# Selective scan of a two-layer adaLN block: TensorE turns the next state's increments ahead of the step's sum

## The reference, cut to what matters

```python
def _selective_scan(u, dt, A, Bm, Cm, Dvec):
    dA = jnp.exp(dt[..., None] * A)
    dBu = dt[..., None] * Bm[:, :, None, :] * u[..., None]
    def step(h, xs):
        dA_t, dBu_t, C_t = xs
        h = dA_t * h + dBu_t
        y = jnp.einsum('bdn,bn->bd', h, C_t)
        return (h, y)
    ...
    return jnp.swapaxes(ys, 0, 1) + u * Dvec
# per layer, after the scan:
    y = y * _silu(z)
    return jnp.einsum('bld,od->blo', y, W_out)
```

## Time and profile before

| what | value |
|---|---|
| median of 3 runs | 775.03 us (768.9 to 779.73) |
| the profiled execution | 776.74 us, span 774.8 us |
| busy over the span | TensorE 83%, VectorE 76%, ScalarE 64%, GpSimd 59% |
| scans, line 1644 | 128, 289.6 us in two groups |
| sums, line 1130 | 512 matmuls, 239.1 us |
| increments, line 1150 | 688 transposes, 91.8 us in two groups |
| C multiplication, line 468 | 128, 301.9 us in two groups |

### The profile page before, as it was taken

The page is one execution under the profiler, slowest core; times in us unless marked ns, Lnnn a source line. Parts: engine busy times, 40 slices in busy tenths (PEclk is TensorE's granted clock), DMA queues, the critical chain, the costliest instruction groups (busy, mean ns, idle before and its releaser), DMA issues. The chain is left out here.

```text
span 774.8 us, 8846 instructions
## 1 busy us (share of the span) xinstructions
PE 642.5 (83%) x2913; PEld 394.4 (51%) x2913; DVE 589.9 (76%) x799; ACT 496.1 (64%) x931; POOL 456.3 (59%) x260
## 2 busy tenths in 40 slices
PE   4946677796699999999986699999999962399993
PEld 2344456432445565555532445565555551389992
DVE  6794986554799999999765799999999858844521
ACT  3553334468799988889668799988989543033321
POOL 1236653100388989879700398989879715058866
PEclk9885877679699999999999699999999965599998
DMA  5000000000223222323100223223322181013333
GB/s 194 0 3 1 0 1 0 1 2 7 80 81 104 89 95 85 106 91 93 48 3 9 78 84 102 88 98 85 104 93 93 46 300 54 1 22 42 39 32 27
DMA packets 30780, 48.05 MB, mean 62 GB/s; under 512 B 3736, under 2 KB 12328, under 8 KB 30224
## 3 DMA queue, kind: packets, MB, share of 16 engines
q1 hardware_dynamic: 25600, 44.45, 18.0%
q0 software_dynamic: 5136, 3.05, 3.6%
HBM read 42.98 MB, written 4.49 MB: 61 GB/s over the span
## 5 line engine op out<-in xcount | busy, mean ns | idle before, releaser
L468 POOL TENSOR_TENSOR hc_all<-hs_all,c_row 128x1024 f32<-128x1024 f32 x88 | 207.3, 2368 | 133.2 <-DVE hs_all L1644 129.9
L1130 PE MATMUL ps<-hc_all,ident 128*128 128x512 f32 x512 | 239.1, 598 | 3.8 <-POOL hc_all L468 2.7
L1644 DVE TENSOR_TENSOR_SCAN hs_all<-da,ps 128x1024 f32<-128x1024 f32 x88 | 198.2, 2271 | 17.1 <-ACT da L794 9.6
L794 ACT ACTIVATE da<-big,a_neg 128x511 f32<-128x511 f32 x256 | 169.2, 709 | 30.5 <-DVE w_ffn L1644 27.6
L1130 PEld LDWEIGHTS ps<-hc_all,ident 128*128 128x128 f32 x512 | 90.2, 192 | 87.5 <-issue 74.2
L468 POOL TENSOR_TENSOR hc_all<-w_ffn,c_row 128x1024 f32<-128x1024 f32 x40 | 94.6, 2365 | 31.7 <-DVE w_ffn L1644 31.7
L1644 DVE TENSOR_TENSOR_SCAN w_ffn<-da,ps 128x1024 f32<-128x1024 f32 x40 | 91.4, 2284 | 3.8 <-ACT da L794 0.9
L1150 PE MATMUL ps<-ident,dbu 128*128 128x128 f32 x464 | 61.6, 276 | 10.5 <-ACT dbu L769 5.0
L1150 PEld LDWEIGHTS ps<-ident,dbu 128*128 128x128 f32 x464 | 53.2, 142 | 27.3 <-issue 16.3
L532 POOL DMA_INDIRECT out<-hc_all,hs_all x32 | 52.2, 1632 | 12.0 <-issue 9.2
L1635 DVE TENSOR_TENSOR ps<-big,ps 128x1024 f32<-128x1024 f32 x42 | 50.8, 1210 | 0.6 <-PE ps L1159 0.4
(11 more groups left out here) (281 smaller groups left out, 1029.9 us busy)
## 6 DMA issues: line engine op xcount, KB each, us to landing
c_row<-c_rows SPq DMA_DIRECT2D x128, 256.0 KB, 3.1
tmpA<-w_in SPq DMA_DIRECT2D x2, 1024.0 KB, 7.1
tmpB<-w_in SPq DMA_DIRECT2D x2, 1024.0 KB, 9.8
x_tok<-x_in SPq DMA_DIRECT2D x2, 512.0 KB, 5.5
out<-x_tok SPq DMA_DIRECT2D x1, 1024.0 KB, 11.4
xm_rows<-xn SPq DMA_DIRECT2D x1, 1024.0 KB, 5.0
w_mod<-w_mod_in SPq DMA_DIRECT2D x2, 384.0 KB, 6.3
w_ffn<-w_ffn_in SPq DMA_DIRECT2D x1, 560.0 KB, 7.6
```

The source lines that it names most:

```text
L468: nc.gpsimd.tensor_tensor(hc[:, n % 4, :, :], hs3[HS_BUF[n]].rearrange("p (i s) -> p i s", i=IC), c_row[:, n % 4, :].unsqueeze(1).to_broad ...
L794: ins = nc.scalar.activation(da[:, n % 2, i, 1:S], dtT[:, b, i, 1:S], ACT.Exp, scale=a_neg[:, l, i, n:n + 1])
L1130: mm = nc.tensor.matmul(ps[:, YS + i, :], ident[:], hc[:, n % 4, i, :], start=(n == 0), stop=(n == NS - 1))
L1644: v.tensor_tensor_scan(hs3[HS_BUF[n]], decay, pair.rearrange("p i s -> p (i s)"), 0.0, ALU.mult, ALU.add).then_inc(c_scan, 1)
```

## The change

In the loop over states, TensorE makes the increments of state n + 1 instead of those of state n. From n = LAG on they stand ahead of `add_state` of the same step; below LAG they stand behind it, but ahead of the projection part, the skip and the turn. Nothing is added or taken away on any engine, and the waits in front of each instruction are the same ones.

```diff
-                        if n in BY_TOKEN[l * B + b]:
-                            increment(b, n)
+                        if n >= LAG and n + 1 in BY_TOKEN[l * B + b]:
+                            increment(b, n + 1)
                         if n == LAG:
 
                             after(pe, c_y, l * B + b)
@@ -1185,6 +1185,8 @@
                             add_state(at - LAG, n - LAG)
                         elif b:
                             add_state(at - LAG, NS + n - LAG)
+                        if n < LAG and n + 1 in BY_TOKEN[l * B + b]:
+                            increment(b, n + 1)
                         for part in range(IC + 1):
```

## The result

| what | before | after |
|---|---|---|
| median | 775.69 us (4 runs) | 792.04 us (4 runs, 786.83 to 796.97) |
| ratio | | 1.0205, 95% interval 1.0155 to 1.0255 |
| the profiled execution | 776.74 us, span 774.8 | 786.83 us, span 784.9 |

The change costs 15.9 us by the ratio. The two profiled spans differ by only 10.1 us, because this execution of the changed kernel reached its first scans 5.3 us earlier, on code that the change doesn't touch. So I compare the scanning stages themselves: from the start of scan 1 (of the second state) to the last gate of the layer. That is 185.35 and 181.73 us before, 195.59 and 186.56 us after: +10.24 in layer 0, +4.83 in layer 1, 15.1 us together.

What follows compares the result with a forecast made beforehand. TensorE was taken as the bound: 9.3 us net for six gates, plus 2.0 for the first batches, less 0.9 hidden afterwards, gives +10.4 us, so 775.0 becomes 785.4 us; range 774 to 792.

Steps and rivals of the forecast that it cites:

- What bounds: Scanning stages: TensorE sets the end, idle 7.4 us in 363 us, with VectorE close behind.
- rival A: VectorE is the real bound and gets faster as its waits for increments disappear: 768.4 us, chance 0.08.
- The wait of I(4): Behind six gates, state 4's increments wait for scan 2: 5.9 us in layer 1, 8.4 in layer 0, net 9.3.
- The first batch: First batch of each layer, no gate: state 4's increments wait 1.5 us for scan 2; net +1.0 us per layer.
- one of the signs named for a wrong forecast: After 211 us, matmuls still running at half clock would show the forecast wrong.
- rival C: Start of each layer: the clock stays low, slower by over 2%; 798 us if until state 2's sum; chance 0.12.
- mild form: First batches: clock rising during state 0's sum costs 0.9 us more, taken up by idle before state 10's increments.
- the swallowed ones: Around the gates: seven earlier waits, 3.16 us in brackets, disappear into the new waiting, taking off 5.0 us.
- less 0.45: After the gates: later TensorE idle hides some of the new waiting, -0.9 us over both layers.
- R(5), which the prediction had in time: Behind a gate: state 5's row ends 2.8 us later, at 583.4, but VectorE wants it only from 584.64.
- Costs nothing elsewhere: Other steps: moving increments ahead of a sum swaps two ready pieces, costing nothing while TensorE has a backlog.
- Order and idle gaps: TensorE keeps program order, so ready sums can't pass waiting increments: +10.4 us; 0 if they could.

Runs made afterwards that it cites:

- I(4) alone: Order of before with only the increments of state 4 pulled ahead of the sum of state 0, against the kernel before: ratio 1.0221, +17.2 us.
- a late gate: Changed kernel with VectorE's gate behind scan 2 instead of ahead of it, against the kernel before: ratio 1.0014, +1.1 us.
- The two kernels without I(4): Changed kernel with state 4's increments left behind the sum of state 0: 1.0120; order of before, new only from state 9 in batches 1 to 3: 1.0099.
- layer 0 alone: The new order in layer 0 only, layer 1 keeping the order of before, against the kernel before: ratio 1.0170, +13.2 us.
- the one without part 0: Changed kernel with three projection matmuls of 0.86 us left out of the loop in layer 1, against the kernel before: ratio 1.0258, +20.0 us.
- layer 1 alone: The new order in layer 1 only, layer 0 keeping the order of before, against the kernel before: ratio 1.0053, +4.1 us.
- the kernel with cover in layer 0: Changed kernel with an overwritten 0.86 us matmul added in layer 0 where layer 1 has its first projection part, against the kernel before: 1.0136, +10.5 us.
- the order before with the late gate: Kernel before with VectorE's gate behind scan 2 instead of ahead of it, against the kernel before: ratio 1.0089, +6.9 us.
- the one with R(5) ahead: Kernel before with GpSimd's two line 459 multiplications at step 6 and state 5's row ahead of state 0's sum, against the kernel before: 0.9991, -0.7 us.

## Why the prediction was right, and where it fell short

**What bounds.** Right. TensorE's idle time is what changed in layer 1. VectorE's relief (rival A) turned into longer waits at the gates, from 4.0 to 9.0 us, as told, and into longer waits for decays, from 10.6 to 21.1 us, which the prediction didn't have; neither gave time back.

**The wait of I(4).** Right in place and nearly in size: waits of 1.78 us in layer 1 (told 1.7) and 2.68, 2.84 and 2.84 us in layer 0 (told 2.5), released by scan 2, at all six gates. I(4) alone reproduces the loss, a late gate removes it.

**The first batch.** The sum had +1.0 us per layer. Scan 1 to the first gate grew from 48.82 to 49.81 us in both layers: +0.99. But one of the signs named for a wrong forecast did come: matmuls beyond 211 us at the lower clock. The place of 211 us is 205.7 in the changed kernel, and there I(4) and S(0) still took 1.97 and 2.78 us; over the 10 us from I(2) on, the mean granted clock was 0.65 instead of 0.83 (layer 1: 0.66 instead of 0.83). This is rival C's mild form, and as C had it, the slack before I(10) took it up: I(10) waits 0.89 us, before 0.85. The windows, changed kernel first, layer 0:

```profile
202.00:212.00 10.00, 8.61 (x29) 5.65 (x30) 8.99 (x6) 10.00 (x22) 8.46 (x4) 0.65 0.22 61
```
```profile
207.34:217.34 10.00, 9.98 (x41) 6.46 (x42) 8.99 (x6) 10.00 (x22) 8.46 (x4) 0.83 0.19 58
```

**Layer 1 as a whole.** The terms of the sum for it are 5.9 for three waits, less 0.68 + 0.21 + 2 x 0.27 = 1.4 for the swallowed ones, less 0.45, plus 1.0: 5.0 us. Measured: 4.83.

**Layer 0: the term that was mis-sized.** The same terms give 8.4 - 3.6 - 0.45 + 1.0 = 5.35 us. Measured: 10.24, so 4.9 are missing. The sum priced all pieces behind the wait at full clock. From the start of I(4) to the start of R(5), which follows S(0), it is 2.65 us in layer 1 (588.34 to 590.99); in layer 0 it was 4.30, 4.16 and 3.98 us, 4.5 us more in all. The other 0.4 us is the waits themselves: layer 1's 1.78 us plus the missing part 0 (0.86) would be 2.64, and they were 2.68, 2.84 and 2.84. Why two of them were 0.2 us longer stays open. R(5), which the prediction had in time, now came late there (VectorE idle 0.69, 0.49 and 0.29 us before it multiplies), but TensorE never waited for that. The low clock as a cost stood in the text, as rival C, but at the wrong place: at the first batch, where it cost nothing. That the six waits behind the gates were themselves a risk to the clock I didn't weigh, though the 2.8 us of layer 0 stood in the sum and the clock was seen low after 3.34 us idle.

So the total was +10.4 us told and +15.9 (15.1 by the stages) measured. The median, 792.04, lies 0.04 above the range's upper end of 792; the ratio on the 775.03 of before gives 790.9, inside it. That the range reached so far was in part luck: it did because of a mild C in the first batches, and the cost came at the gates. The ratio of 1.0205 has an interval that spans 2%, so the runs don't tell whether the kernel is slower by more than that.

**"Costs nothing elsewhere".** That swapping two ready pieces costs nothing while TensorE has a backlog holds for the changed kernel: behind the gates none of its other steps waits 0.2 us or more. But it held because the waits at the gates made the backlog. The two kernels without I(4) show it.

**Order and idle gaps.** That a ready sum does not pass a waiting increment is borne out: S(0) had its product and the gate's end by 586.10, yet it starts at 589.27, 0.93 us after I(4) at 588.34. The Trainium skill, "TensorE: Matmul & The Clock Gate", in the table under "Why this matters for your kernels", advises against idle gaps between bursts of matmuls, since the clock falls back. The trace agrees for the gates of layer 0, and the last section has the numbers.

## What to carry to other kernels

Before you move an instruction ahead on an engine that takes its work in order, look up what releases it and what was covering that time: here two pieces (2.15 us) covered a scan, and moving the increment before them turned the cover into idle time. Ask of each new wait on TensorE how long it is, too: in this kernel those of 2.44 us and more at a gate were paid twice, once as idle and once at half clock, and a dummy matmul inside each of the three waits of layer 0 was worth 4.95 us together. And when a removed wait reveals another behind it, undoing "the guilty step" alone does not give the time back.

## What the runs showed of the hardware

TensorE's clock fell at waits that I had priced as idle time alone. Of the waits in dense stretches that I read with a window of 10 us around them, the fifteen of 2.44 to 2.84 us (bracket) had a mean granted clock of 0.83: layer 0's gates in the changed kernel, in the one with layer 0 alone and in the one with I(4) alone, and all six gates in the one without part 0. Those of 1.78 us (layer 1 of the changed kernel, of the one with layer 1 alone and of the one with I(4) alone, and the three of the kernel with cover in layer 0) and those of 2.18, 1.78 and 1.78 us in layer 0 of the order before with the late gate had 1.00. Where it fell, it cost 1.3 to 1.7 us more on I(4) and S(0) in the changed kernel.

It did not always fall while TensorE stood still. In the kernel without part 0, at the gate shown above, it was still at 2.4 GHz up to the start of I(4) at 549.69, and at 1.2 GHz behind it, in the midst of work:

```profile
549.20:549.69 0.49, 0.00 (x0) 0.03 (x1) 0.49 (x2) 0.22 (x1) 0.27 (x2) 1.00 0.45 105
550.00:553.00 3.00, 3.00 (x10) 1.97 (x9) 3.00 (x2) 3.00 (x8) 3.00 (x2) 0.50 0.03 6
```

By the trace's record of the clock the fall came between 0.6 us before and 1.1 us after I(4)'s start over the fifteen places, and in ten of them after it. So a matmul that starts at the full clock behind such a wait may still end at the lower one.

The stretch between the last gate of layer 0 and scan 1 of layer 1 is the same code in the kernel before and the one with R(5) ahead. It took 46.87 us in the profile of the first and 50.20 us in that of the second:

```profile
390.37:437.24 46.87, 35.00 (x86) 13.49 (x84) 25.95 (x34) 34.30 (x53) 2.36 (x1) 0.88 0.10 31
```
```profile
389.50:439.70 50.20, 38.36 (x86) 14.59 (x84) 25.96 (x34) 34.39 (x53) 2.35 (x1) 0.82 0.09 29
```

The other engines' busy times are equal to 0.1 us; TensorE's 86 matmuls took 3.4 us more, at a granted clock of 0.82 instead of 0.88. Where TensorE is used sparsely, the clock comes and goes differently from one execution to the next. Over the fourteen profiles this stretch took 46.87 to 50.34 us. That fits the scatter of one kernel's runs (766 to 782 us for the one before), though no run shows that it makes all of it, and it is why a change confined to dense stretches is read better from the stages than from one run's total.
